# Feed-forward blocks take in their normalisations, and the first attention's head and rotary stage are rearranged

## What is computed

```python
x = x + _L0_attn_ref(_layernorm(x), ...)      # rotary on q and k, 16 heads of 16, causal
x = x + _L0_ffn_ref(_layernorm(x), W1, W2, W3)  # silu(x W1') * (x W3'), Hadamard, W2: here block f0
x = x + _L1_attn_ref(_layernorm(x), ...)
x = x + _L1_ffn_ref(_layernorm(x), ...)         # the same with a 2-of-4 selection: block f1
x = x + _L2_attn_ref(_layernorm(x), W, b)       # a recurrence
x = x + _L2_ffn_ref(_layernorm(x), ...)         # eight experts: block f2
x = x + _L3_attn_ref(_layernorm(x), ...)
x = x + _L3_ffn_ref(_layernorm(x), ...)         # ternary weights, rms norm: block f3
```

## Time and profile before

| | us |
|---|---|
| median of three runs | 978.56 |
| lowest, highest | 976.45, 984.68 |
| the profiled execution, whole | 982.71 |
| its span | 980.9 |
| PE busy, DVE busy, ACT busy, POOL busy | 796.5, 629.0, 389.4, 174.7 |
| granted PE clock, mean of the span | 0.906 |

### The profile page before, as it was taken

The page is one execution under the profiler, slowest core; times in us unless marked ns, Lnnn a source line. Parts: engine busy times, 40 slices in busy tenths (PEclk is TensorE's granted clock), DMA queues, the critical chain, the costliest instruction groups (busy, mean ns, idle before and its releaser), DMA issues. The chain is left out here.

```text
span 980.9 us, 12463 instructions
## 1 busy us (share of the span) xinstructions
PE 796.5 (81%) x4306; PEld 511.2 (52%) x4306; DVE 629.0 (64%) x1328; ACT 389.4 (40%) x660; POOL 174.7 (18%) x224
## 2 busy tenths in 40 slices
PE   1616899998499787999986997669899999658797
PEld 1514333425388663344335686555556666446676
DVE  6687978835664577789626788453156773165675
ACT  4023266674431252466764442451122222143553
POOL 1534111221200040022210000103202221100143
PEclk9858799999799997899997999778999999978899
DMA  6107320000000076200006100595201110120001
GB/s 229 63 3 227 98 65 2 2 2 1 0 1 1 16 247 205 66 2 2 2 1 124 3 1 1 199 387 190 87 11 44 49 44 33 65 92 1 1 3 41
DMA packets 49523, 63.96 MB, mean 65 GB/s; under 512 B 12502, under 2 KB 34774, under 8 KB 49462
## 3 DMA queue, kind: packets, MB, share of 16 engines
q1 hardware_dynamic: 47590, 58.05, 19.2%
q0 software_dynamic: 1872, 5.13, 1.5%
HBM read 50.30 MB, written 15.51 MB: 67 GB/s over the span
## 5 line engine op out<-in xcount | busy, mean ns | idle before, releaser
L800 DVE TENSOR_REDUCE at1mx<-at1ps_s 128x1 f32<-128x512 f32 (+3 forms) x152 | 90.4, 656 | 17.9 <-PE at1ps_s L702 10.8
L800 DVE TENSOR_REDUCE at0mx<-at0ps_s 128x1 f32<-128x512 f32 (+3 forms) x152 | 90.7, 656 | 17.4 <-PE at0ps_s L702 10.4
L780 ACT ACTIVATE at1probs<-at1ps_e 128x1024 f32<-128x1024 f32 (+3 forms) x96 | 73.8, 809 | 45.8 <-PE at1ps_e L723 45.5
L780 ACT ACTIVATE at0probs<-at0ps_e 128x1024 f32<-128x1024 f32 (+3 forms) x96 | 73.8, 809 | 45.6 <-PE at0ps_e L723 45.3
L1063 PE MATMUL f2ps<-gu_raw,f2xT_b 128*128 x184 | 82.9, 593 | 1.0 <-ACT f2xT_b L1138 1.0
L1156 ACT ACTIVATE f2sg<-f2ps 128x512 f32<-128x512 f32 x31 | 18.5, 597 | 137.2 <-PE f2ps L1063 100.9
L699 PE MATMUL at0ps_s<-ks,qs 96*128 96x512 bf16 (+3 forms) x192 | 58.1, 364 | 5.9 <-DMA ks<-scratch 4.4
L699 PE MATMUL at1ps_s<-ks,qs 96*128 96x512 bf16 (+3 forms) x192 | 56.9, 353 | 6.8 <-DMA ks<-scratch 4.6
L1232 DVE TENSOR_TENSOR f2h<-f2sg,f2ps 128x512 f32<-128x512 f32 x31 | 21.3, 686 | 60.8 <-ACT f2sg L1156 27.0
L1063 PEld LDWEIGHTS f2ps<-gu_raw,f2xT_b 128*128 128x128 f32 x184 | 34.8, 190 | 35.5 <-issue 34.4
L1283 POOL DMA_INDIRECT rows_out<-xT,f2x_in x23 | 29.0, 1259 | 127.9 <-DVE xT L1220 127.9
(11 more groups left out here) (395 smaller groups left out, 1797.8 us busy)
## 6 DMA issues: line engine op xcount, KB each, us to landing
gu_raw<-in_L_ffn_w_gate_up SPq DMA_DIRECT2D x8, 1024.0 KB, 13.0
scratch<-parts SPq DMA_DIRECT2D x8, 768.0 KB, 3.9
qs<-scratch SPq DMA_DIRECT2D x48, 128.0 KB, 2.8
ks<-scratch SPq DMA_DIRECT2D x48, 128.0 KB, 2.8
dn_raw<-in_L_ffn_w_down SPq DMA_DIRECT2D x8, 512.0 KB, 12.2
f2x_in<-slots_in SPq DMA_DIRECT2D x23, 129.0 KB, 2.1
slots_in<-in_c_empty SPq DMA_DIRECT2D x1, 2944.0 KB, 17.1
traw<-in_L_ffn_w_gate_up SPq DMA_DIRECT2D x1, 2048.0 KB, 12.3
```

What stands on the lines that cost most here:

```text
L780: act.activation(probs[:, slots(v), 0:n], ps_e[:, v % SCORE_PAIRS, :, 0:n], ACT.Exp, scale=HD ** -0.5)\
L800: dve.tensor_reduce(mx[:, p % 2, lo // CH, j:j + heads, t], rows_of, AX.X, ALU.max).then_inc(s_red, 1)
```

## The change

1. A class `HalfNorm` does the normalisation inside `ffn_stage` and `sparse_ffn_stage`, by halves of four tiles: n1, n3 and n7 are stages no more. Its transposes go through the last bank pair of the projection's PSUM.
2. In f0, GpSimd begins splitting the next weights after h of unit 7.
3. n0 makes one round. Since the first result has mean 0 and variance v/(v+1e-5), one root of v(1+1e-5) + 1e-10 gives both; the row length is made from v. x comes in four DMAs in n0 itself, each pair of tiles waited for apart, and the block ahead of n0 is gone. SyncE issues 11 other DMAs in n0 (what n0 and the rotary stage need) and the other 13 in the rotary stage.
4. In the rotary stage TensorE adds the bias by a product of a row of ones with the bias row into each tile; VectorE's own products read PSUM; ScalarE copies chunks 1 to 3 out of PSUM for GpSimd.

```diff
@@ norm_stage, VectorE @@
+            for i in range(PAIRS + 3):
+                if i < PAIRS:
+                    if arrived is not None:
+                        dve.wait_ge(arrived[i], 16)
+                    for t in (2 * i, 2 * i + 1):
+                        number["sums", t] = signal(dve.bn_stats(st[:, t, :], m.x[:, t, :]))
...
+                n = signal(dve.tensor_scalar(length[:], mv[:, :, 1], 1e-5, None, ALU.add))
                 dve.wait_ge(done, n)
+                n = signal(dve.reciprocal(length[:], length[:]))
+                dve.wait_ge(done, n)
+                dve.tensor_tensor(length[:], length[:], mv[:, :, 1], ALU.mult).then_inc(std_ready, 1)
@@ rotary_stage @@
             pe.wait_ge(*w_ready)
+            pe.wait_ge(*bias_ready)
             for t in range(T):
+                pe.matmul(ps[:, t, :], m.one_row[:], bias[0:1, :], start=True, stop=False, skip_group_check=True)
                 for part, x in enumerate((xq, xk)):
...
-            def take(c):
-
-                dve.wait_ge(mm, (c + 1) * CT)
-                i = ps[:, c * CT:c * CT + CT, :]
-                dve.tensor_tensor(chunk(raw, c).rearrange("p t h d -> p t (h d)"), i,
-                                  bias.unsqueeze(1).to_broadcast([P, CT, 2 * D]), ALU.add).then_inc(z_s, 1)
...
+            def take(c):
+
+                act.wait_ge(mm, (c + 1) * CT)
+                act.activation(chunk(raw, c - 1).rearrange("p t h d -> p t (h d)"), ps[:, c * CT:c * CT + CT, :], ACT.Copy)\
+                   .then_inc(z_s, 1)
+
             for i in range(CHUNKS + 1):
+                if i < CHUNKS - 1:
+                    take(i + 1)
@@ class HalfNorm @@
+    def turn(self, pe, m, half):
+        if half:
+            pe.wait_ge(self.ready, KD)
+        for j, t in enumerate(self.tiles(half)):
+            if t % 2:
+                pe.wait_ge(self.xn_a, t // 2 + 1)
+            else:
+                pe.wait_ge(self.xn_v, t // 2 + 1)
+            for k in range(KD):
+                ins = pe.transpose(self.room[:, k, j * P:j * P + P], self.xn[:, t, k * P:k * P + P], m.ident[:])
+        ins.then_inc(self.turned, 1)
+
+    def high(self, act, m, half):
+        act.wait_ge(self.turned, half + 1)
+        for k in range(KD):
+            act.activation(m.xp[0][:, k, half * CH:half * CH + CH], self.room[:, k, :], ACT.Copy).then_inc(self.high_s, 1)
+
+    def low(self, dve, m, half):
+        for k in range(KD):
+            cols = slice(half * CH, half * CH + CH)
+            dve.wait_ge(self.high_s, half * KD + k + 1)
+            dve.tensor_tensor(m.xp[1][:, k, cols], self.room[:, k, :], m.xp[0][:, k, cols].bitcast(F32), ALU.subtract)\
+               .then_inc(self.ready, 1)
@@ ffn_stage, TensorE @@
+                nm.turn(pe, m, 0)
...
+                    if f == 0:
+                        pe.wait_ge(nm.ready, KD * (c + 1))
...
                     ins.then_inc(gu, 1)
+                    if n == 0:
+                        nm.turn(pe, m, 1)
@@ ffn_stage, ScalarE @@
+                act.activation(nm.warm[:], m.eps5[:], ACT.Sqrt, bias=m.eps5[:])
+                if raw:
                     act.wait_ge(*ready(p, buf, True))
+                    high(p, buf, 0)
+                nm.roots(act, m, 0)
+                nm.odd(act, m, 0)
+                nm.roots(act, m, 1)
+                if raw:
+                    high(p, buf, 1)
+                nm.high(act, m, 0)
+                act.activation(nm.warm[:], m.eps5[:], ACT.Silu)
+                nm.odd(act, m, 1)
@@ ffn_stage, VectorE @@
+                nm.statistics(dve, m, 0)
+                nm.statistics(dve, m, 1)
+                nm.even(dve, m, 0)
+                if raw:
+                    low(p, buf, 0)
+                nm.low(dve, m, 0)
+                if raw:
+                    low(p, buf, 1)
+                nm.even(dve, m, 1)
@@ ffn_stage, GpSimd @@
             def _(pool):
+                pool.wait_ge(hs, ft)
                 side_work(pool)
```

More of the change, by code:

```diff
@@ L140, in _ @@
             number = {}
[L141 to L172, removed]
@@ L390, in _ @@
                        .then_inc(std_s, 1)
+        @block.sync
+        def _(sp):
+            for dst, src, s in loads:
+                sp.dma_start(dst, src, allow_slow_non_contiguous=True).then_inc(s, 16)
 PARTS_OF = ((0, 0, 0, 1, 1, 2), (0, 1, 2, 0, 1, 0))
@@ L1344, in project_down @@
                     pe.wait_ge(router.ex, 1)
+                if f == 0 and c == OB - 1:
+                    pe.wait_ge(nm.ready, KD * NC)
                 if f == 0 and not (is_first and c < OB):
@@ L1482, in work @@
                     router.split(dve)
-                if raw and is_first:
-                    for f in range(ft if sets > 1 else 2):
-                        low(p, buf, f)
+                nm.statistics(dve, m, 0)
[7 more added lines that the diff above has]
+                nm.even(dve, m, 1)
                 for n in range(U):
@@ L1602, in _ @@
                     n = b * 4 + j
+                    if blk == 0 and j == 0:
+                        pe.wait_ge(nm.ready, KD * (c + 1))
                     if n < H // P:
@@ L1737, in _ @@
             add(NC - 1)
+        @block.sync
+        def _(sp):
+            for dst, src, s in loads:
+                sp.dma_start(dst, src).then_inc(s, 16)
 @stage
@@ L2031, in build @@
                     v_all = sb("v_all0", [P, GROUPS, T, GH, 32], stack=l0)
-                    first = on("consts", [(m.ident[:], ap["c_ident"]), (above32[:], ap["c_above"])])
+                    x_rows = ap["x"].rearrange("(t p) d -> p t d", p=P)
+                    first = sum((on("x%d" % q, [(m.x[:, 2 * q:2 * q + 2, :], x_rows[:, 2 * q:2 * q + 2, :])])
+                                 for q in range(T // 2)), [])
+                    first += on("ident", [(m.ident[:], ap["c_ident"])])
                     first += on("l0", [(t[:], column(ap["L0_attn_" + n])) for t, n in
@@ new lines, in build @@
+                    first += on("l0b", [(l0b[:, 0:D], wide(ap["L0_attn_bq"])), (l0b[:, D:3 * D], wide(ap["L0_attn_bkv"]))])
+                    first += on("above", [(above32[:], ap["c_above"])])
+                    then = on("ln", [(lng[:].rearrange("p w f -> p (w f)"), ap["ln_g_rows"]),
+                                     (lnb[:].rearrange("p w f -> p (w f)"), ap["ln_b_rows"]),
+                                     (l0b[:, 3 * D:4 * D], wide(ap["L0_attn_bo"]))])
+                    then += on("wo0", [(wa0[:, :, 3 * D:], rows(ap["L0_attn_Wo"]))])
```

234 lines of the change are left out of this document (153 added, 81 removed).

## The result

The changed kernel takes 968.22 us (median of 13 runs, 961.78 to 977.3) against 978.75 us for the kernel before in the same job (13 runs, 976.45 to 984.68): ratio 0.9875, 95% interval 0.9845 to 0.9906, so 9 to 15 us faster. The prediction said 961.0 with a range of 954 to 970. The direction is right and the time is inside the range, but of the 17.6 us of the sum only 12.2 came by the ratio, so about a third did not.

A forecast was written before the change was run, and what follows sets the result against it. No engine fills the span, so each edit was priced where it stands in the timeline: 10.7 - 0.6 + 6.0 + 1.8 - 0.3 = 17.6 us off the median 978.56 gives 961.0, range 954 to 970.

The forecast's parts named there:

- Head: Up to the rotary stage's start: one normalisation round and fewer DMAs move that start from 24.18 to 13.5, gaining 10.7 us.
- Rotary: Rotary stage: GpSimd starts 1.5 us later, its chain takes 20.1; 46.1 us against 45.4, counted as -0.6 us.
- with 0.83 or 1.7 more on each tile they take 12.5 to 13.5: Rotary stage: TensorE's first four tiles, 9.3 us, plus the bias product at full or half clock; lower end taken.
- the slow start: Rotary stage: half clock at first adds about 2.6 us to the 6.7 us of TensorE's first four tiles.
- the first rival: Rotary stage takes most of the head's gain back: all four tiles at half clock, 8 us more, 969; chance 0.15.
- The rule of the Trainium skill: Rotary stage: only VectorE instructions with two SBUF inputs block GpSimd's SBUF reads; moving L319 frees nothing, otherwise some 3 us.
- f0: Opening of f0: unit 2 at 18.5 us from the first statistics in place of 24.54, gaining 6.0 us.
- GpSimd at unit 8: f0: GpSimd's moved split may hold VectorE, counted as nothing; rival that it blocks, 4.9 us more, 966, chance 0.08.
- f1: Opening of f1: unit 2 at 17.4 us from the first statistics against 19.37, gaining 1.8 us.
- f3: Opening of f3: unit 2 at 14.8 us from the first statistics against 14.52, counted as -0.3 us.
- Scaling to the median: Whole kernel: the profiled execution, 982.71 us, lies 4.15 above the median 978.56, so the sum is taken from the median.
- The rival that the clock stays low in the feed-forward units: Feed-forward units: short transposes keep the clock at 1.2 GHz, about 2.7 us per further unit, up to 1004; chance 0.05.

The follow-up runs named there:

- the repeat: The changed kernel run once more, unchanged, for its spread and a second trace: 965.72 us against 979.57 for the kernel before, ratio 0.9863.
- the kernel without any bias: Changed kernel with the bias product left out, so bq and the key half of bkv are not added: 962.94 us, ratio 0.9833.
- the one wait alone: Kernel before with one line added, holding GpSimd's weight parts (L70, L72) until f0's eighth h: 974.73 us, ratio 0.9958.
- n7 apart: Changed kernel with the last normalisation, n7, a stage of its own again ahead of f3: 968.15 us, ratio 0.9879.
- the old rotary arithmetic: Changed kernel with VectorE adding the bias as it copies for GpSimd, no bias product and no ScalarE copy: 965.02 us, ratio 0.9860.
- 128 rows: Changed kernel with the bias product over 128 rows (weights 1/128) in place of one row: 966.86 us, ratio 0.9874.
- both repairs: Changed kernel with the bias product over 128 rows and n7 a stage of its own: 964.04 us against 980.88, ratio 0.9845.

## Why the prediction was right or wrong

**Head: right.** 13.68 and 14.11 for a forecast 13.5, by its own steps: SyncE done at 8.4 (8.3), normalised at 9.8 (9.7), written at 13.2 (13.2).

**Rotary: the mechanism right, the term mis-sized.** It said: TensorE's first four tiles, ScalarE's copy, GpSimd's chain, VectorE's tail. The chain took 19.9 us (20.1) and the tail 12.2 (12.2). The step that failed is "with 0.83 or 1.7 more on each tile they take 12.5 to 13.5". A tile at full speed takes 2.98 us against 1.73 without the product, so 1.25 more and not 0.83; at half speed 5.7 against 3.5 (24.18 to 27.72 in the kernel before). And the slow start, put at about 2.6 us more than at full speed, cost 3.0 in the repeat (two tiles in 8.99 us, not 5.96) and 8.1 in the profiled execution (three in 17.08, not 8.94). GpSimd started at +21.3 and +16.2, not +13.8, and the stage lost 8.0 and 2.9 us, not 0.6. That is the first rival (969, given 0.15): the profile showed nearly all of it in one of two traces and a third in the other. The mistake was to read how long TensorE had been slow before under a product of another shape and to hold it for a constant.

The rule of the Trainium skill weighed there (SBUF — State Buffer, section "SBUF: two separate sides") held: without the addition beside it GpSimd's chain got 1.0 us shorter (20.0 against 21.0 with it), not 3. That came with the first of its chunks, which now runs after VectorE has finished its own. In the kernel without any bias GpSimd starts earlier, VectorE's L333 beside it takes 2.16 us in place of 1.22, and the chain takes 20.9, with no addition at all.

**f0: right.** 7.0 us from n1 to n2 (6.0 forecast), of which the one wait alone brings 4.1. **GpSimd at unit 8: right**, that rival fell: VectorE's two operations took 4.4 us longer together, and TensorE had no idle row.

**f1: the opening right, the rest not.** Unit 2 at +17.43 (17.4), in the changed kernel:

```profile
519.05 1.41 DVE L1319 BATCH_NORM_STATS2 n3st<-x 128x6 f32<-128x256 f32 x4 [0.32 <-PEq L861]
```
```profile
536.48 0.50 PE L1729 MATMUL f1ps_g<-x3hi,f1part_gu 128*128 128x512 f32 x1 [0.36 <-DVE f1part_dn L1793]
```

But from n3 to n4 the stage takes 96.2 to 96.5 us in four traces and 94.2 to 94.7 in the six others with n3 inside, against 97.2 before: 0.8 or 2.9 gained. In each of the four the granted clock dips between 24 and 48 us behind the first statistics, in none of the six; it dips there too in all four traces with n3 apart, the kernel before's among them (window of the changed kernel, 30 to 42 us behind the first statistics, then the same of the old rotary arithmetic):

```profile
549.05:561.05 12.00, 9.84 (x37) 0.86 0.00 0
```
```profile
536.30:548.30 12.00, 9.51 (x40) 1.00 0.00 1
```

**f3: sign right, size not.** Unit 2 at +14.97 (14.8), 0.45 later than before. Then some 1.6 more at the chunk boundary, where the clock came back low, and 0.7 between the issue of the last store and the end (5.0 us against 4.3, in all traces with n7 inside and in none of the others; why is open): -2.7 in all. The prediction ended each sum at unit 2. It had read "from unit 2 on TensorE has no gaps and sets the pace" in f0 and carried it to f1 and f3, though the kernel before's own trace has a pause there in both (2.2 us at 560.48 and this one in f3):

```profile
955.38 1.18 PE L1349 MATMUL f3ps_o<-f3part_dn,f3hpart 128*128 128x256 f32 x8 [2.32 <-DVE x L1474]
```

**The sum.** Changed parts in the traces: 10.5 - 8.0 + 7.0 + 0.8 - 2.7 = 7.6 us in the profiled execution, and 10.1 - 2.9 + 7.4 + 0.7 - 2.7 = 12.6 in the repeat; about 10 in the mean, beside 12.2 by the ratio and 17.6 forecast. The parts that nothing touched make the rest in each (-2.1 and +6.5 against the kernel before's trace, spans 5.5 and 19.1 apart). Nearly all of the shortfall is the rotary term and f3. **Scaling to the median** was sound in size: the kernel before's profiled execution lay 4 us above its median, and it had 192.9 us from f2's first unit to n6 where every other trace has 189.3 to 190.3. The rival that the clock stays low in the feed-forward units did not come: in f0 unit 0 ran at half speed for 3.8 us (255.46 to 259.3) and unit 1 at full speed.

What stays open: why the 4 to 9 us that 128 rows take off the rotary stage show in medians as nothing (966.9 beside 965.7 and 968.2) or as 4 us at most (both repairs beside n7 apart, 964.0 and 968.2; by the ratios 3.3). The changes of the clock behind it (the second attention, f1) differ from execution to execution of the same kernel, with 4 to 13 runs of each the medians are sure to some 3 to 4 us, and no experiment here steers them.

## What to carry to other kernels

Where an engine's first products after a pause hold up a chain, price them with their own shape and at half speed for the whole of it as the bound, and see whether another engine that waits anyway can do the work: here the rotary stage was 0.7 us shorter with VectorE's bias addition than with TensorE's product, at full speed in both. When two traces are compared for such a start, look first whether the clock was at the same level when it began. A block between VectorE and GpSimd is best found in the trace by one operation that takes several times its usual duration, and holding GpSimd back until there is slack was one line for 4 us. Do not end the sum at the last edited instruction: an opening that moves can put a later pause where the clock comes back low.

## What the runs showed of the hardware

- A float32 product over one row of 512 columns is no cheaper than one over 128 rows: 1.05 us from its start to the next product at full speed against 0.86, and with its neighbours a tile of 2.98 us against 2.59.
- The view of windows prints a clock of 1.00 where the trace holds no clock record. In the changed kernel's trace the first record is the rise at 30.7 us, and up to it the products took twice as long. The window from 13.60 to 17.60, first of the changed kernel (7 records), then with 128 rows (13 records, behind that trace's first rise at 12.0):

```profile
13.60:17.60 4.00, 3.92 (x7) 1.00 0.28 79
```
```profile
13.60:17.60 4.00, 3.71 (x13) 1.00 0.24 63
```

  Both print 1.00. So the clock column has to be held against the products' own durations before a stage is called fast, above all ahead of the first record.
- After a pause of 2.3 us (n7 inside f3) the granted clock came back at 0.57 to 0.60 over 4 us in all seven traces, and at 1.00 after the same pause in all seven with n7 apart. By the stage's units this cost 1.6 us.
- The same code in the second attention runs with a stretch of granted clock 0.57 in some executions and 1.00 in others, 4.2 us apart.
